# Hybrid attention kernel: the gate G is added by VectorE in PSUM instead of by two identity matmuls, and softmax sums are inverted as rows instead of through a DMA transpose

## What is computed

```
L1 = einsum('bhnd,bhmd->bhnm', l2norm(q1), l2norm(k1)) * cos_scale
L2 = einsum('bhnd,bhmd->bhnm', l2norm(q2), l2norm(k2)) * cos_scale
G  = tanh(delta_gain.reshape(1, H, 1, 1) * (L1 - L2))
A1 = softmax(L1 + G);  A2 = softmax(L2 - G)
y  = einsum('bhnm,bhmd->bhnd', A1 - lambda_full * A2, v)
y  = y * rsqrt(mean(y * y, axis=-1) + RMS_EPS) * subln_weight
```

## Time and profile before

| | |
|---|---|
| median of 8 runs | 6040.45 us |
| the profiled execution | 6035.35 us |
| its span on the slowest core (core 7) | 6033.8 us |
| spans of the 8 cores | 5950.4 to 6033.8 us |
| busy share of the span: PE, DVE, ACT, POOL | 48%, 24%, 24%, 5% |
| attention A's groups on core 7 | 924.8 to 2109.9 and 2520.1 to 3706.8 us of the span |
| attention B's groups on core 7 | 4478.5 to 4934.1 and 5176.6 to 5625.4 us of the span |

### The profile page before, as it was taken

The page is one execution under the profiler, slowest core; times in us unless marked ns, Lnnn a source line. Parts: engine busy times, 40 slices in busy tenths (PEclk is TensorE's granted clock), DMA queues, the critical chain, the costliest instruction groups (busy, mean ns, idle before and its releaser), DMA issues.

```text
span 6033.8 us, 35983 instructions; the slowest of 8 cores (5950.4 to 6033.8 us)
## 1 busy us (share of the span) xinstructions
PE 2880.8 (48%) x9536; PEld 759.7 (13%) x9536; DVE 1456.7 (24%) x2432; ACT 1464.2 (24%) x1528; POOL 319.3 (5%) x535
## 2 busy tenths in 40 slices
PE   0012436666555443466556654352446544655625
PEld 0000111111111011111111111110111111111201
DVE  1335330000111133200100111515431225222241
ACT  0000113444444311144444441000003320233000
POOL 0100000000000000000000000000001100011000
PEclk9985556677777756777877686686776667766858
DMA  2000000000000000000000001000100000000101
GB/s 87 8 9 11 11 18 3 6 6 6 6 8 6 7 13 14 14 6 6 6 6 7 6 6 27 6 13 2 40 17 5 6 15 23 12 6 5 30 3 68
DMA packets 107520, 83.52 MB, mean 14 GB/s; under 512 B 45086, under 2 KB 94750, under 8 KB 105022
## 3 DMA queue, kind: packets, MB, share of 16 engines
q1 hardware_dynamic: 79710, 55.07, 3.0%
q0 software_dynamic: 27616, 26.14, 2.3%
HBM read 70.08 MB, written 10.98 MB: 13 GB/s over the span
## 4 chain that ended last, share of the span: by engine, by line
PE 34%; DVE 19%; DMA 19%; ACT 14%; issue 11%; DVEq 1%; ACTq 0%; POOLq 0%; SPq 0%; PEldq 0%; POOL 0%
ACT a_E L119 8%; PE pj_p L119 7%; PE a_pY L119 6%; PE a_pL L119 5%; DMA scrb<-xpb 4%; PE a_pD L119 3%; PE a_ps L119 3%; PE f_p L119 3%; DMA b_rb<-scrb 3%; DMA scr<-rr 3%; DVE tmpf L119 3%; PE tm_pv L119 2%; ACT qrows L119 2%; DMA wqb<-qout 2%; DMA xpf<-scr 2%
## 5 line engine op out<-in xcount | busy, mean ns | idle before, releaser
L119 PE MATMUL a_pY<-a_E,aV 128*128 128x512 bf16 x1024 | 393.0, 474 | 811.7 <-ACT a_E L119 811.6
L119 ACT ACTIVATE a_G<-a_pD,gvec 128x512 bf16<-128x512 f32 x512 | 352.7, 689 | 1197.2 <-PE a_pD L119 1188.7
L119 ACT ACTIVATE a_E<-a_pL,ccol 128x1024 bf16<-128x1024 f32 x512 | 569.6, 1112 | 94.0 <-PE a_pL L119 90.8
L119 ACT ACTIVATE b_E<-b_pS,ccol 128x1024 bf16<-128x1024 f32 (+1 forms) x320 | 312.3, 987 | 1121.3 <-PE b_pS L119 1119.3
L119 PE MATMUL b_pYa<-b_E,bV 128*65 128x512 bf16 (+1 forms) x320 | 145.0, 453 | 366.5 <-DVE b_E L119 262.4
L119 PE MATMUL ln_px<-ln_xb,ones_col 128*1 128x512 bf16 x128 | 74.4, 581 | 468.6 <-DVEq L119 468.6
L119 POOL DMA_DIRECT2D scr<-rr x160 | 81.3, 508 | 4023.2 <-DVEq L119 3914.5
L119 PE MATMUL a_pD<-aQ,aKn 128*128 128x512 bf16 x512 | 253.6, 495 | 44.4 <-DVEq L119 23.5
L119 ACT ACTIVATE qrows<-qrows 1x4096 bf16<-1x4096 bf16 x32 | 115.7, 3617 | 588.6 <-DVEq L119 587.1
L119 PE MATMUL a_pL<-a_G,id_bf 128*128 128x512 bf16 x512 | 257.9, 504 | 0.0
L119 PE MATMUL a_pL<-a_G,idn_bf 128*128 128x512 bf16 x512 | 253.7, 495 | 0.0
(11 more groups left out here) (151 smaller groups left out, 3170.0 us busy)
## 6 DMA issues: line engine op xcount, KB each, us to landing
a_rb<-scrb POOLq DMA_DIRECT2D x32, 256.0 KB, 3.9
pj_wf<-WqkT SPq DMA_DIRECT2D x32, 256.0 KB
out<-resid SPq DMA_DIRECT2D x8, 1024.0 KB, 10.2
resid<-xT SPq DMA_DIRECT2D x4, 1024.0 KB, 11.9
resid<-xT POOLq DMA_DIRECT2D x4, 1024.0 KB, 12.5
pj_wf<-WqT SPq DMA_DIRECT2D x16, 256.0 KB
pj_wf<-WkT SPq DMA_DIRECT2D x16, 256.0 KB
tm_wvhf<-WvT SPq DMA_DIRECT2D x16, 256.0 KB
```

The source lines that it names most:

```text
L119: r = getattr(eng, name)(*args, **kw)
```

## The change

1. The identity matrices, their two loads and casts, and the pair of identity matmuls of every chunk (512 pairs) are gone. DVE adds G to the first bank of `a_pL` and subtracts it from the second, in place in PSUM, behind tanh.
2. ACT's order becomes tanh of chunk j, then exp of the same chunk j; the exp behind the loop is gone.
3. The rows of sums are inverted by DVE where they are, in one partition: RECIPROCAL over 1 x 512, twice per group in A and in B, followed in A by a product with lambda. Two DMAs write the two bf16 rows to `scrb`, and the broadcast read stays. The trip through `scr` and `xpf` is gone.
4. The row of squares: ACT takes its square root out of `a_pD` at chunk 6, between tanh and exp; DVE inverts it (1 x 512) at chunk 8, and POOL writes and broadcasts it then.

```diff
@@ head @@
-    ld(S, id_f[:], di["ident"])
-    ld(S, idn_f[:], di["identn"])
...
@@ attention A, one chunk @@
                     P.matmul(pL2[sB][:, 0, :], Kh[hl][0:64, jsl], Qh[h][0:64, tsl],
-                             start=True, stop=False, tile_position=(0, 0))
+                             start=True, stop=True, tile_position=(0, 0))
...
-                    if jg >= 1 and j >= 1:
-                        sGp = (jg - 1) & 1
-                        P.matmul(pL2[sGp][:, 0, :], id_bf[:, :], Gb[sGp][:],
-                                 start=False, stop=True, tile_position=(0, 0))
-                        P.matmul(pL2[sGp][:, 1, :], idn_bf[:, :], Gb[sGp][:],
-                                 start=False, stop=True, tile_position=(0, 0),
-                                 inc="s_pa")
...
                     if j == 6 and prev is not None:
-                        b.wait("vector", "s_pv", b.cnt["s_pv"])
-                        b.wait("vector", "s_gd")
-                        V.tensor_copy(rr[0:1, 0:QT], pD[0:1, :])
...
+                        b.wait("scalar", "s_pv")
+                        A.activation(rrow2[0:1, 0:QT], pD[0:1, :], AF.Sqrt,
+                                     scale=1.0 / 128.0, bias=ccol[0:1, 0:1],
+                                     inc="s_sq")
...
-                    if j >= 1:
-                        sEp = (jg - 1) & 1
-                        b.wait("scalar", "s_pa", aff(pa0, jg - 1))
-                        b.wait("scalar", "s_pv", at(pv, jg - 3))
-                        A.activation(Eb[sEp][:, :, :], pL2[sEp][:, 0:2, :], AF.Exp,
-                                     bias=ccol[:, 1:2], inc="s_x")
+                    b.wait("scalar", "s_pa", aff(pa0, jg))
+                    b.wait("scalar", "s_pv", at(pv, jg - 2))
+                    A.activation(Eb[sB][:, :, :], pL2[sB][:, 0:2, :], AF.Exp,
+                                 bias=ccol[0:1, 0:1] if False else ccol[:, 1:2],
+                                 inc="s_x")
+
+                    b.wait("vector", "s_g", aff(gc0, jg))
+                    b.wait("vector", "s_lm", aff(lm0, jg))
+                    V.tensor_add(pL2[sB][:, 0, :], pL2[sB][:, 0, :], Gb[sB][:])
+                    V.tensor_sub(pL2[sB][:, 1, :], pL2[sB][:, 1, :], Gb[sB][:],
+                                 inc="s_pa")
...
+                        if j == 8:
+                            b.wait("vector", "s_sq", at(sq, xi - 1))
+                            V.reciprocal(rrb[64:65, 0:QT], rrow2[0:1, 0:QT])
...
+                            ld(G, d_scrb[a_sc + 2 * QT:a_sc + 3 * QT],
+                               rrb[64:65, 0:QT], sem="s_gd")
...
@@ attention A, end of a group @@
-                ld(G, d_scr[a_tp:a_tp + QT], rr[0:1, 0:QT], sem="s_gd")
-                ld(G, d_scr[a_tp + QT:a_tp + 2 * QT], rr[32:33, 0:QT], sem="s_gd")
-                b.wait("gpsimd", "s_gd")
-                ld(G, xpf[:, 0:8],
-                   _ap(d_scr, a_tp, [[4, 128], [QT, 2], [1, 4]]), sem="s_gd")
-                b.wait("vector", "s_gd")
-                V.reciprocal(xpb[:, 0:8], xpf[:, 0:8])
+                V.reciprocal(rrb[0:1, 0:QT], rr[0:1, 0:QT])
+                V.reciprocal(rrb[32:33, 0:QT], rr[32:33, 0:QT])
                 b.drain("vector")
...
-                ld(G, _ap(d_scrb, a_sc, [[4, 128], [QT, 2], [1, 4]]),
-                   xpb[:, 0:8], sem="s_gd")
+                ld(G, d_scrb[a_sc:a_sc + QT], rrb[0:1, 0:QT], sem="s_gd")
+                ld(G, d_scrb[a_sc + QT:a_sc + 2 * QT], rrb[32:33, 0:QT], sem="s_gd")
```

More of the change, by code:

```diff
@@ L818, in build_program @@
                         while len(sq) < xi:
                             sq.append(b.cnt["s_sq"])
-                    if j == 7 and prev is not None:
-                        b.wait("gpsimd", "s_sq", at(sq, xi - 1))
-                        ld(G, d_scr[a_tp + 2 * QT:a_tp + 3 * QT], rr[0:1, 0:QT],
-                           sem="s_gd")
-                        b.wait("gpsimd", "s_gd")
-                        ld(G, xpf[:, 8:12],
-                           _ap(d_scr, a_tp + 2 * QT, [[4, 128], [1, 4]]),
-                           sem="s_gd")
@@ L828, in build_program @@
-                    if j == 8 and prev is not None:
-                        b.wait("scalar", "s_gd")
-                        A.activation(xpf[:, 8:12], xpf[:, 8:12], AF.Sqrt,
-                                     scale=1.0 / 128.0, bias=ccol[:, 0:1],
-                                     inc="s_se")
-                    if j == 9 and prev is not None:
-                        b.wait("vector", "s_se")
-                        b.wait("vector", "s_gd")
-                        V.reciprocal(xpb[:, 8:12], xpf[:, 8:12])
-                        b.drain("vector")
-                        b.inc_last("vector", "s_ve")
@@ L871, in build_program @@
                 jg = xi * NKC + NKC - 1
-                b.wait("tensor", "s_g", aff(gc0, jg))
-                P.matmul(pL2[jg & 1][:, 0, :], id_bf[:, :], Gb[jg & 1][:],
-                         start=False, stop=True, tile_position=(0, 0))
-                P.matmul(pL2[jg & 1][:, 1, :], idn_bf[:, :], Gb[jg & 1][:],
-                         start=False, stop=True, tile_position=(0, 0),
-                         inc="s_pa")
-                b.wait("scalar", "s_pa", aff(pa0, jg))
-                b.wait("scalar", "s_pv", at(pv, jg - 2))
-                A.activation(Eb[jg & 1][:, :, :], pL2[jg & 1][:, 0:2, :], AF.Exp,
-                             bias=ccol[:, 1:2], inc="s_x")
                 b.wait("tensor", "s_x", aff(x0, jg))
@@ L934, in build_program @@
                      tile_position=(0, 0), inc="s_pv")
-            b.wait("vector", "s_pv", b.cnt["s_pv"])
-            b.wait("vector", "s_gd")
-            V.tensor_copy(rr[0:1, 0:QT], pD[0:1, :])
+            b.wait("scalar", "s_pv")
+            A.activation(rrow2[0:1, 0:QT], pD[0:1, :], AF.Sqrt, scale=1.0 / 128.0,
+                         bias=ccol[0:1, 0:1], inc="s_sq")
+            b.wait("vector", "s_sq")
+            V.reciprocal(rrb[64:65, 0:QT], rrow2[0:1, 0:QT])
             b.drain("vector")
@@ L940, in build_program @@
             b.wait("gpsimd", "s_ve")
[L941 to L954 removed]
+            ld(G, d_scrb[a_sc + 2 * QT:a_sc + 3 * QT], rrb[64:65, 0:QT], sem="s_gd")
             b.wait("gpsimd", "s_gd")
@@ L1222, in build_program @@
                 b.inc_last("vector", "s_ev")
-                b.wait("gpsimd", "s_ev")
-                ld(G, d_scr[a_tp:a_tp + QT], rr[64:65, 0:QT], sem="s_gd")
-                ld(G, d_scr[a_tp + QT:a_tp + 2 * QT], rr[0:1, 0:QT], sem="s_gd")
-                b.wait("gpsimd", "s_gd")
-                ld(G, xpf[:, 0:8],
-                   _ap(d_scr, a_tp, [[4, 128], [QT, 2], [1, 4]]), sem="s_gd")
-                b.wait("vector", "s_gd")
-                V.reciprocal(xpb[:, 0:8], xpf[:, 0:8])
+                V.reciprocal(rrbB[64:65, 0:QT], rr[64:65, 0:QT])
+                V.reciprocal(rrbB[0:1, 0:QT], rr[0:1, 0:QT])
                 b.drain("vector")
```

61 lines of the change are left out of this document (15 added, 46 removed).

## The result

The changed kernel takes 5928.33 us (median of 11 runs, 5925.17 to 5943.2) beside 6032.84 us of the kernel before (32 runs): a ratio of 0.9821, 95% interval 0.9795 to 0.9848, so 1.8% faster. The prediction was 5985 us, 0.8% under its profiled execution. The profiled execution of the kernel after takes 5928.47 us, 106.9 less than the one before; 50 of these were predicted.

A forecast was written before the change was run, and what follows sets the result against it. Neither engine full: PE and ACT take turns, exp standing behind the next tanh. On core 7: first group -18.0, fifteen groups -5, second half -18.3, ends -10, B -11, head -3.6, sum -66; slowest span 5983, forecast 5985 us, range 5900 to 6150.

The forecast's parts named there:

- A chunk: Attention A: exp, tanh, two DVE additions and signals sum to 3.33 us whatever TensorE's clock, with PE hidden.
- dearer additions: Rival, chance 0.12: in-place PSUM additions take longer than copies out; every 0.1 us per instruction costs 102 us.
- cheaper signals: Rival, chance 0.18: ways between ACT and DVE take 0.10 us each; 72 us less, a total of 5913 us.
- The end of a group: Attention A: DVE's reciprocals become exposed; 13.4 us from last exp's end to next exp, 11.2 us per group on the path.
- dearer reciprocal: Rival, chance 0.18: 512 columns take 3.95 or 4.7 us instead of 3.4; a total of 6055 or 6151 us.
- Chunk 4 and chunk 8: Attention A: DVE's y instructions expose 1.2 us at the former; the third reciprocal exposes 1.8 at the latter.
- Chunk 6: Attention A: square root waits for ones matmul and PV block, then two table loads; 3.5 us exposed per group.
- The first group of a half: Attention A: only chunks and the way to its copies, 54.9 us from its first tanh.
- The head: Program's start: two loads of 1.83 us leave the chain, -3.6 us.
- Ends of the halves: Attention A: shorter trips, partly offset by a reciprocal; 5 us gained per half, between 0 and 7.
- PE late: Rival, chance 0.05: PE's 0.3 us cover at 1.2 GHz fails; 0.1 late on half the chunks costs 26 us, totalling 6011.
- B: the step that failed: Group ends in attention B: trip to the broadcast 0.7 us earlier per group, 32 groups, 0 to -22, taken as -11.

The follow-up runs named there:

- B's rows alone: Kernel before, with two row reciprocals and two row writes replacing the trip through `scr` and `xpf` in attention B only: 5995.75 us, ratio 0.9902.
- the run with the use moved: Changed kernel with B's use of `b_rb` moved from chunk 3 to the group's last chunk: 5849.18 us, ratio 0.9633.

## Why the prediction was right, and where it was wrong

- *A chunk*: 3.33 us predicted, 3.31 measured, at a clock of 0.50. Additions 1.30 for two (1.29). Right. The rivals of dearer additions and cheaper signals fall.
- *The end of a group*: 13.4 predicted, 13.6 measured. Two reciprocals take 6.70 (6.8 predicted). The rival of a dearer reciprocal falls, and with it the reading of the Trainium skill ("VectorE: DVE Perf Modes", "First, the fixed hardware budget") as 8 cycles a column: 3342 ns for 512 columns, against 4.4 us by that estimate.
- *Chunk 4 and chunk 8*: 1.2 and 1.8 predicted; 1.3 and 1.8.
- *Chunk 6*: 3.5 predicted, 4.1 measured (7.39 less 3.31). From the ones matmul's start to the first table load it was 2.15 us, where about 1.5 and a signal of 0.17 were taken; no row stood behind the 1.5, and the stage ran at 1.2 GHz. A group came to 71.75 us, not 71.0, so over 30 groups the cost was taken 22 us too low.
- *The first group of a half*: 54.9 predicted, 54.9 measured. *The head*: -3.6 predicted, -6.8 measured on the mean core; what the rest is was not followed. *Ends of the halves*: 5 each predicted, 7.4 measured on the mean core, just above the bound of 7.
- *PE late*: the cover of 0.3 us held (tanh's idle time for `a_pD` is 87 us in all); two more matmuls break it, as shown.
- *B: the step that failed.* "So 0.7 us earlier per group, 32 times if each is on the path, none if none: 0 to -22, and I take -11." Measured: -59 on the mean core, -58 on core 7. Two numbers in that sentence were wrong. The 0.7 (0.8 by its own terms: 7.4 to 7.1 and 5.5 to 5.0) came from one trip of A, in which DVE was held 7.2 us, one of the shortest. Over the 256 groups of B on all cores, the time from the end of the copies to the use of `b_rb` has a mean of 18.9 us before (8.1 of it to the end of the inversion, up to 12.7; 5.4 to the broadcast's issue; 5.3 to its use) and 17.2 after (7.0, 5.2 and 5.1): 1.65 less per group, more than half of it in the hold, and not 0.7. And all 32 groups are on the path, not half, because the masks (in groups of 4 chunks the next copies) stand behind the wait at chunk 3. 32 times 1.65 are 53 of the 59 us; the rest was not followed. The run with B's rows alone shows that B gains this by itself, and the table by group length and the run with the use moved show that the wait is on the path.
- *The slowest core.* The prediction expected the slowest of core 3's kind at 5974 to 5992. Core 3 alone gained 95.8 us, and in B 93.4, where its trips had been longest (19.9 us on the mean, 17.3 after). The 28 us of vanished spread were not in the sum. The step "A will take about equally long on all cores" was right; that B would as well had been left out.

The sign and the mechanism in A were right; the size was missed by one term, B, whose own bounds (0 to -22) do not hold it. That the run still lies in the stated range of 5900 to 6150 is luck: the range reached below 5930 for cheaper signals, which did not come. By its own chances the prediction thought a change within 1% the likeliest (0.38) and gave a gain of more than 1%, which came, 0.35.

## What to carry to other kernels

Read the length of a DMA round trip over all its instances and cores, not from one row, and find out what stands behind its wait in the queue of the waiting engine: that decides on how many groups it counts. A long instruction costs its full length as soon as the engine has become part of the chain; the same 6.7 us were free while PE added the gate. When a change moves little, look for the chain that the rest now forms: taking exp out of the way of tanh and DVE's waits out of the way of the additions and of B's masks gave, all together, nine times what the change did.
